# Slot numbers of 8 bits in place of words in the count stage of a graph network kernel

## The chip, the core and the metric

The kernel runs on one core of a Trainium2 chip. The metric is the time of the whole program on that core in microseconds (us), the median of three runs. TensorE is called PE here, VectorE DVE, ScalarE ACT, GpSimd POOL, SyncE SP. Each engine has a sequencer, which also runs the register instructions of its program; in the rows these stand under the engine's name with a q behind it (PEldq is the sequencer of PE, which issues weight loads and matmuls both).

## What is computed

Four graph layers run one after the other on 3125 nodes of 128 features, over 103125 edges that are sorted by destination. The part that matters here is what all the first three layers share: a sum over the edges of a node.

```python
edge_index = jnp.stack([src, dst])
h = jnp.maximum(_layernorm(x, axis=-1), 0.0)
x = x + _L0_gnn_ref(h, edge_index, ...)     # segment_sum of gated messages
x = x + _L1_gnn_ref(h, edge_index)          # three rounds: segment_sum(x[src], dst) / count
x = x + _L2_gnn_ref(h, src, dst, ...)       # segment_sum(feat[src], dst) / degree, two linears
x = x + _L3_gnn_ref(h, edge_index, edge_attr_32, ...)   # attention over the edges
```

For the first three layers the kernel builds once a matrix of counts (how many edges run from node s to node d) and then multiplies with it. The stage that builds this matrix is the one that is changed.

## The kernel before

**Stages.** `tables` works out the index tables on DVE with a little help of PE. `count_matrix` builds the counts. Then come layer 0, layer 1, layer 2 (matmuls with the counts) and layer 3 (projection, attention over edge groups, feed-forward). A stage is a block, and the next begins when all engines have left it.

**The count stage.** The edges lie in 806 tiles of 128, the nodes in 625 windows of 5 destinations. A step takes one tile and one window; there are 1431 steps. DVE makes the one-hot operands of 16 steps with two comparisons (line 617): one of the source's low 7 bits, 128 wide, one of the pair of window place and high bits, 125 wide. PE multiplies the two, with 128 rows of weights and 125 columns (line 646), and adds the product into a slot of 128 columns in PSUM. Which slot is data: the window of a step depends on the edges. Eight steps are a stride (`STRIDE`), so there are 179 strides. PSUM has 32 slots, in four pairs of banks (`PAIRS`). Per stride PE first sends two matmuls with one column of zeros (line 624, `clear`), which reset a pair of banks ahead, and ACT reads one pair of banks out into the counts (line 653).

**Places in registers.** `CountTables.places` works out on DVE, at the end of the tables stage, for each step its slot offset in PSUM (slot number times 128 columns) and for each stride the pair to clear (pair number times 1024). They lie in `c_place`, for each three strides (`AHEAD`) 24 + 3 values and one of padding: 28 words of 32 bits. PE's sequencer reads those 28 words into 28 registers with one TENSOR_LOAD (line 114, called from `values`), 60 times in the stage. The registers hold for the three strides that follow. Before each matmul a register instruction (FUSED_REGOPS) turns the value into an address. For line 646 it has two operations, times 4 bytes and plus the base of PSUM; for line 624 three, plus 511 or 1023, times 4, plus the base. ACT loads its own words, one of a stride, 8 at a time (line 657).

**Order and waits.** Everything is written out, with no scheduler. PE waits before a stride j for the read-out of stride j-2 (`copied`), and before each second stride for the one-hots of DVE (`hots`). DVE may be three chunks of 16 steps ahead (`ring`). ACT waits for the matmuls of the stride (`counted`).

Of the kernel before, what the change touches and what calls it, by code (L numbers as in the profile page):

```python
# [7 lines left out]
BF16 = mybir.dt.bfloat16  # L8
I32 = mybir.dt.int32
I16 = mybir.dt.int16  # L10
ALU = mybir.AluOpType
ACT = mybir.ActivationFunctionType
AX = mybir.AxisListType
ENGINE = mybir.EngineType
# [13 lines left out]
SLOT = 128  # L28
STRIDE = 2 * IN_BANK
PAIRS = 4  # L30
AHEAD = 3
F16_SCALE = 4096.0

# [112 lines left out]
class Path:  # L147
# [29 lines left out]
    def vector(self, e, v):  # L177
# [7 lines left out]
        e.wait_ge(v.sem, v.at(t))  # L185
        e.tensor_tensor(ends[:, :], ends[:, :], self.tile_no[:, :], ALU.add).then_inc(*v.up())
        t = v.n
# [25 lines left out]
class CountTables:  # L213
# [7 lines left out]
    def __init__(self, k, scope):  # L221
        s = k.s
        n, cols = s.csteps, s.nb * s.w
        self.k = k

        def sb(name, shape, dt=F32):
            return k.sb(scope, name, shape, dt, "right")
        self.key, self.low = sb("c_key", [P, n + 1], F16), sb("c_low", [P, n + 1], F16)

        self.fetches = -(-s.strides // AHEAD)
        self.words = -(-AHEAD * (STRIDE + 1) // 4) * 4
        self.place = sb("c_place", [1, self.fetches, self.words], I32)
        self.out = sb("c_out", [1, self.fetches * AHEAD], I32)
        self.lows, self.keys = sb("low_table", [P, P, 2], F16), sb("key_table", [P, cols, 2], F16)

    def stage(self, scope):
        k, s, n = self.k, self.k.s, self.k.s.csteps
        self.kb = -(-s.tiles // P)
        self.last = s.tiles - (self.kb - 1) * P  # L240
        self.cuts = [(lo, min(n, lo + 397)) for lo in range(0, n, 397)]
        kb, tiles = self.kb, s.tiles

        def sb(name, shape, dt=F32):
            return k.sb(scope, name, shape, dt)
        self.src, self.dst = sb("src_rows", [P, 2, kb, P], I32), sb("dst_rows", [P, 2, kb, P], I32)
        self.tile_no, self.step = sb("tile_no", [P, tiles]), sb("step", [P, 16])
        self.iota, self.far = sb("iota", [P, P]), sb("far", [P, s.nb * s.w])
        self.number = sb("number", [P, n], F16)
        self.part = sb("part", [P, 2, kb, P], I32)  # L250
        self.diff = sb("diff", [P, 4, kb, P], F16)
        self.dst_diff = sb("dst_diff", [P, kb, P])
        self.end, self.ends = sb("end", [P, kb], I32), sb("ends", [P, kb])
        self.before = sb("before", [P, kb, n], F16)
        self.shifts, self.near = sb("shifts", [P, n]), sb("near_key", [P, 2, 397])
        self.ones = sb("ones", [P, 1], F16)
        strides = self.fetches * AHEAD
        whole = strides * STRIDE
        self.window = sb("c_window", [1, whole], I32)
        self.fill, self.early = sb("c_fill", [1, strides], I32), sb("c_early", [1, strides])  # L260
        self.clear, self.pair, self.column = (sb(x, [1, strides], I32) for x in ("c_clear", "c_pair", "c_column"))
        self.blank, self.dst_here, self.src_here, self.numbers_here, self.tables_here = (k.flag(x) for x in (
            "c_blank", "c_dst_here", "c_src_here", "c_numbers_here", "c_tables_here"))
        self.before_ready, self.summed, self.lows_kept, self.emptied = (k.flag(x) for x in (
            "c_before", "c_summed", "c_lows_kept", "c_emptied"))
        self.v = k.flag("c_vector")
# [91 lines left out]
    def places(self, e):  # L358

        s, v = self.k.s, self.v
        assert STRIDE * PAIRS == 32 and SLOT == 128
        wide = STRIDE * s.w
        every = AHEAD * STRIDE
        e.memset(self.place[:, :, every + AHEAD:], 0).then_inc(*v.up())
        e.tensor_scalar(self.place[:, :, 0:every], self.window[:, :].rearrange("p (a b) -> p a b", b=every),
                             STRIDE * PAIRS - 1, 7, ALU.bitwise_and, ALU.logical_shift_left).then_inc(*v.up())
        e.tensor_scalar(self.fill[:, :], self.window[:, ::STRIDE], 3, None, ALU.logical_shift_right).then_inc(*v.up())
        t = v.n
        e.wait_ge(v.sem, v.at(t))  # L370
        for to, more in ((self.clear, 1), (self.pair, PAIRS - 1)):
            e.tensor_scalar(to[:, :], self.fill[:, :], float(more), None, ALU.add).then_inc(*v.up())
        e.tensor_scalar(self.early[:, :], self.fill[:, :], 1.0, float(wide * (s.fills - 1)),
                                 ALU.is_lt, ALU.mult).then_inc(*v.up())
        t = v.n
        e.wait_ge(v.sem, v.at(t))
        e.tensor_scalar(self.place[:, :, every:every + AHEAD], self.clear[:, :].rearrange(
            "p (a b) -> p a b", b=AHEAD), PAIRS - 1, 10, ALU.bitwise_and, ALU.logical_shift_left).then_inc(*v.up())
        e.tensor_scalar(self.pair[:, :], self.pair[:, :], PAIRS - 1, 16, ALU.bitwise_and, ALU.logical_shift_left).then_inc(*v.up())
        e.scalar_tensor_tensor(self.early[:, :], self.fill[:, :], float(wide), self.early[:, :],  # L380
                                        ALU.mult, ALU.add).then_inc(*v.up())
        t = v.n
        e.wait_ge(v.sem, v.at(t))
        e.tensor_scalar(self.column[:, :], self.early[:, :], -float(wide), None, ALU.add).then_inc(*v.up())
        t = v.n
        e.wait_ge(v.sem, v.at(t))
        e.tensor_tensor(self.out[:, :], self.column[:, :], self.pair[:, :], ALU.bitwise_or).then_inc(*v.up())
# [30 lines left out]
def tables(k, c):  # L418
# [6 lines left out]
    with ExitStack() as scope:  # L425
# [7 lines left out]
        k.e_rel = k.dram("e_rel", (P, 4 * s.padded))  # L433
        k.e_rel_rows = k.dram("e_rel_rows", (s.padded, 2 * wide), I16)

# [149 lines left out]
def count_matrix(k, c, counts, room):  # L585
# [4 lines left out]
    s, w = k.s, k.s.w  # L590
    keep, ring, cols = c.KEEP, 3, s.nb * s.w
# [3 lines left out]
    with ExitStack() as scope:  # L595
        def sb(name, shape, dt=F32):
            return k.sb(scope, name, shape, dt)
        lows = room.bitcast(F16)[:, 0:ring * keep * P].rearrange("p (r n v i) -> p r n v i", r=ring, n=keep // 2, i=2)
        keys = sb("keys", [P, ring, keep // 2, cols, 2], F16)
        none = sb("none", [P, 512], F16)  # L600
        consts, hots, cleared, counted, copied = (k.flag(x) for x in (
            "count_constants", "hots", "cleared", "counted", "copied"))
        flat = k.psum[:, :, :].rearrange("p b n -> p (b n)")

        with k.nc.Block() as block:
            @block.vector
# [14 lines left out]
            @block.tensor  # L621
            def _(e):
                def clear(bank):
                    return e.matmul(bank, none[:, 0:P], none[:, 0:1], start=True, stop=True, skip_group_check=True)
                words = c.place[0:1, :, :].rearrange("p a b -> p (a b)")
                last_slot = (STRIDE * PAIRS - 1) * SLOT
                e.wait_ge(consts.sem, consts.at(1))
                for i in range(BANKS):
                    e.matmul(k.bank[i], none[:, 0:P], none[:, :], start=True, stop=True, skip_group_check=True)
                    last = clear(k.bank[i][:, 511:512])  # L630
                last.then_inc(*cleared.up())
                for j in range(s.strides):
                    if j % AHEAD == 0:
                        at = j // AHEAD * c.words
                        fetched = k.values(ENGINE.PE, words, at, at + c.words, last_slot)
                    place = fetched[j % AHEAD * STRIDE:(j % AHEAD + 1) * STRIDE]
                    ahead = fetched[AHEAD * STRIDE + j % AHEAD].with_bounds(min_val=0, max_val=(PAIRS - 1) * 1024)
                    if j >= 2:
                        e.wait_ge(copied.sem, copied.at(j - 1))
                    for i in range(2):  # L640
                        clear(flat[:, 512 * i + 511:][:, bass.ds(ahead, 1)])
                    if j % per == 0:
                        e.wait_ge(hots.sem, hots.at(2 * (j // per) + 2))
                    for i in range(j * STRIDE, min(s.csteps, (j + 1) * STRIDE)):
                        hot = (slice(None), i // keep % ring, i % keep // 2, slice(None), i % 2)
                        last = e.matmul(flat[:, bass.ds(place[i - j * STRIDE], cols)], lows[hot], keys[hot], start=False, stop=True,  # L646
                                        skip_group_check=True)
                    last.then_inc(*counted.up())

# [1530 lines left out]
```

## Time and profile before

| what | value |
|---|---|
| three runs, median (lowest to highest) | 2661.04 us (2653.04 to 2667.34) |
| the profiled execution, by the clock of the runs | 2660.26 us |
| its span in the trace | 2658.5 us |
| PE busy, of the span | 1727.1 us (65%) |
| DVE busy | 1524.0 us (57%) |
| ACT busy | 940.4 us (35%) |
| the count stage, from the first to the last clearing matmul | 75.3 to 414.6 us |

Busy time counts work on data only. Register instructions and the loading of registers are not in it, so an engine whose sequencer is reading registers looks idle; such a gap is put down either to "issue" or to whichever semaphore happened to come last. The trace still has these instructions, and a view of one source line shows their number and their duration.

### The profile page before, as it was taken

How to read it: one execution, taken by the hardware profiler on the slowest of the kernel's cores; microseconds unless marked ns; L12 is line 12 of the kernel's file. 1: busy time of each engine (PE TensorE's matmuls, PEld its weight loads, DVE VectorE, ACT ScalarE, POOL GpSimd, SP SyncE). 2: the span in 40 equal slices, each digit the busy share in tenths (PEclk: the TensorE clock that was granted, in tenths of full speed). 3: DMA queues.
4: the chain of work that ended last, by engine and by line, in shares of the span. 5: the costliest groups of instructions: out<-in, count | busy, mean ns of one | idle time of the engine just before them, and what ended most of it. 6: DMA issues, size and time to landing. Idle time of an engine off the chain costs nothing. (4 is left out here: it accounts for less than half of the span.)

```text
span 2658.5 us, 34091 instructions
## 1 busy us (share of the span) xinstructions
PE 1727.1 (65%) x10020; PEld 1399.0 (53%) x10020; DVE 1524.0 (57%) x3280; ACT 940.4 (35%) x2179; POOL 891.8 (34%) x871
## 2 busy tenths in 40 slices
PE   4666665995599777443566665756565566666665
PEld 2455553553488665232455554645455555555663
DVE  5666664774432333843565665656656666566786
ACT  0455554673334131300223323324233233242455
POOL 1000000000000000076666655666656566566600
PEclk9555555998799889677777867778878777787777
DMA  2000001000024000132323323333223233223211
GB/s 65 20 1 1 1 1 27 1 0 24 25 59 126 1 1 8 43 97 70 80 72 77 79 70 75 73 75 78 75 75 79 76 78 78 70 71 82 69 26 29
DMA packets 131762, 136.86 MB, mean 51 GB/s; under 512 B 28321, under 2 KB 101634, under 8 KB 131586
## 3 DMA queue, kind: packets, MB, share of 16 engines
q0 software_dynamic: 27776, 60.71, 10.1%
q1 hardware_dynamic: 103810, 73.98, 9.8%
q8 instruction: 90, 1.47, 0.2%
q14 instruction: 86, 0.70, 0.1%
HBM read 129.67 MB, written 4.92 MB: 51 GB/s over the span
## 5 line engine op out<-in xcount | busy, mean ns | idle before, releaser
L1618 POOL DMA_INDIRECT rows<-x_l,src x856 | 875.7, 1023 | 966.4 <-DMA rows<-L_gnn_b 449.7
L1686 PE MATMUL psum<-both,node_hot 128*128 128x144 f32 x1712 | 326.1, 349 | 324.8 <-DVE both L1880 216.1
L1686 PEld LDWEIGHTS psum<-both,node_hot 128*128 128x128 f32 x1712 | 287.3, 238 | 353.4 <-issue 319.8
L1633 PE MATMUL psum<-w_e,edges 128*128 128x272 f32 x856 | 330.7, 472 | 132.5 <-issue 80.5
L1635 PEld LDWEIGHTS psum<-x_r,hot 128*128 128x128 f32 x1712 | 319.4, 226 | 100.3 <-issue 50.3
L1635 PE MATMUL psum<-x_r,hot 128*128 x1712 | 328.4, 316 | 43.0 <-issue 42.4
L1786 DVE TENSOR_SCALAR hot<-rel_row,place 128x512 f32<-128x512 int16 x214 | 103.9, 486 | 340.9 <-remote 289.5
L1743 ACT ACTIVATE apart<-iota,minus_rel 128x128 f32<-128x128 f32 x828 | 261.9, 386 | 0.1
L653 ACT ACTIVATE counts<-psum (+1 forms) x181 | 181.4, 1002 | 186.9 <-PE psum L646 117.0
L1898 DVE TENSOR_TENSOR acc<-acc,psum 128x144 f32 x428 | 128.7, 301 | 198.1 <-remote 135.4
L1633 PEld LDWEIGHTS psum<-w_e,edges 128*128 128x128 f32 x856 | 165.5, 233 | 140.5 <-issue 96.8
L1019 PE MATMUL psum<-halves,counts 128*128 128x257 f16 (+1 forms) x1875 | 214.0, 276 | 28.4 <-PEq L1036 24.5
L1039 POOL MEMSET halves<- 128x6425 f16 x1 | 5.5, 5456 | 651.6 <-SPq L1036 651.6
L1019 PEld LDWEIGHTS psum<-halves,counts 128*128 128x128 f16 (+1 forms) x1875 | 185.7, 99 | 56.8 <-issue 25.5
L646 PE MATMUL psum<-keys,x 128*128 128x125 f16 x1431 | 201.8, 285 | 0.5
L617 DVE TENSOR_TENSOR x<-low_table,c_low 128x2048 f16<-128x2048 f16 x90 | 109.6, 1218 | 123.2 <-PE psum L646 121.3
L1739 ACT ACTIVATE both<-weight 128x64 f32<-128x64 f32 x214 | 52.7, 246 | 344.8 <-remote 264.5
L646 PEld LDWEIGHTS psum<-keys,x 128*128 128x128 f16 x1431 | 149.0, 105 | 25.4 <-issue 1.5
L1793 DVE TENSOR_TENSOR z<-psum,rows 128x544 f32<-128x544 f32 x214 | 153.0, 715 | 9.1 <-issue 9.1
L1806 DVE TENSOR_REDUCE alpha<-z 128x32 f32<-128x544 f32 x214 | 152.5, 712 | 1.6 <-issue 0.5
L1799 DVE SCALAR_TENSOR_TENSOR z<-z,att 128x512 f32<-128x512 f32 x214 | 146.6, 685 | 1.1
L1880 DVE TENSOR_TENSOR both<-rows,weight 128x512 f32<-128x512 f32 x214 | 143.9, 680 | 3.5 <-issue 2.6
(299 smaller groups left out, 2101.9 us busy)
## 6 DMA issues: line engine op xcount, KB each, us to landing
rel_row<-e_rel_rows SPq DMA_DIRECT2D x107, 256.0 KB
rows<-x_l,src POOLq DMA_INDIRECT x856
edges<-edge_t SPq DMA_DIRECT2D x428, 32.0 KB
edge_part<-edge_t SPq DMA_DIRECT2D x22, 576.0 KB
x_r<-x_l SPq DMA_DIRECT2D x1, 1632.0 KB
new<-e_new_before SPq DMA_DIRECT2D x12, 128.0 KB
new<-e_new_behind SPq DMA_DIRECT2D x12, 128.0 KB
x_l<-xl SPq DMA_DIRECT2D x4, 340.0 KB
```

What stands on the lines that cost most here:

```text
L646: last = e.matmul(flat[:, bass.ds(place[i - j * STRIDE], cols)], lows[hot], keys[hot], start=False, stop=True, skip_group_check=True)
L653: return e.activation(counts[:, :, column].rearrange("p h (a j) -> p h a j", j=w), pair.rearrange("p b (a n) -> p (b a) n", n=SLOT)[:, 0:f ...
L1019: last = e.matmul(ps, counts[:, i, b * P:b * P + rows], halves[:, i, :], start=i == 0, stop=i == s.nb - 1)
L1618: e.indirect_dma_start(rows[:, g % ring, j * ROW:(j + 1) * ROW], None, k.xl, bass.IndirectOffsetOnAxis(ap=src[:, at:at + 1], axis=0)).then ...
L1633: e.matmul(pair[:, j // 2, :], edges[:, r, :], w_e[:, j:j + 2, :].rearrange("p j f -> p (j f)"), start=True, stop=False)
L1635: final = e.matmul(pair[:, j // 2, j % 2 * ROW:(j % 2 + 1) * ROW], hot[:, two, j * P:(j + 1) * P], node_rows[j // 2], start=False, stop=j ...
L1686: final = e.matmul(to, near_hot[:, at, j, :], both[:, at, j, :], start=j % 2 == 0, stop=j % 2 == 1)
L1743: e.activation(apart[:, u % 2, j, :], iota[:, :], ACT.Abs, bias=minus_rel[:, 4 * u + j:4 * u + j + 1]).then_inc(*far.up())
L1793: e.tensor_tensor(z[:, g % 2, :].rearrange("p (b f) -> p b f", b=2), pair_of(g), rows_at(g).rearrange("p (b f) -> p b f", b=2), ALU.add).t ...
L1799: e.scalar_tensor_tensor(heads, heads, 0.0, att_of(k, 4), ALU.max, ALU.mult).then_inc(*leaky.up())
L1806: e.tensor_reduce(alpha[:, b.two, :, g - b.first, :], z[:, g % 2, :].rearrange("p (v h c) -> p v h c", v=4, h=HEADS), AX.X, ALU.add).then_ ...
L1880: e.tensor_tensor(both[:, at, :, 0:D].rearrange("p v (h c) -> p v h c", c=CH), rows_at(u).rearrange("p (v h c) -> p v h c", v=4, h=HEADS)[ ...
```

## The change

`c_place` becomes a tile of bytes. A step has its slot number, 0 to 31, a stride the number of its pair, 0 to 3, and three strides take 24 + 3 bytes and 5 of padding (`FETCH` = 32). PE loads 32 bytes with one TENSOR_LOAD, into 32 registers, again 60 times. The multiplication by 128, or by 1024, that the table held is now made by the sequencer, since PSUM is seen as slots and as pairs.

```diff
+FETCH = 32
...
-        self.words = -(-AHEAD * (STRIDE + 1) // 4) * 4
-        self.place = sb("c_place", [1, self.fetches, self.words], I32)
+        assert AHEAD * (STRIDE + 1) <= FETCH
+        self.place = sb("c_place", [1, self.fetches, FETCH], U8)
...
-        e.tensor_scalar(self.place[:, :, 0:every], self.window[:, :].rearrange("p (a b) -> p a b", b=every),
-                             STRIDE * PAIRS - 1, 7, ALU.bitwise_and, ALU.logical_shift_left).then_inc(*v.up())
+        e.tensor_scalar(self.slot[:, :], self.window[:, :], STRIDE * PAIRS - 1, None, ALU.bitwise_and).then_inc(*v.up())
...
-        e.tensor_scalar(self.place[:, :, every:every + AHEAD], self.clear[:, :].rearrange(
-            "p (a b) -> p a b", b=AHEAD), PAIRS - 1, 10, ALU.bitwise_and, ALU.logical_shift_left).then_inc(*v.up())
+        e.wait_ge(v.sem, v.at(u))
+        e.tensor_copy(self.place[:, :, 0:every], self.slot[:, :].rearrange("p (a b) -> p a b", b=every)).then_inc(*v.up())
+        e.tensor_scalar(self.clear[:, :], self.clear[:, :], PAIRS - 1, None, ALU.bitwise_and).then_inc(*v.up())
...
+        e.tensor_copy(self.place[:, :, every:every + AHEAD], self.clear[:, :].rearrange("p (a b) -> p a b", b=AHEAD)).then_inc(*v.up())
...
-        flat = k.psum[:, :, :].rearrange("p b n -> p (b n)")
+        slots = k.psum[:, :, :].rearrange("p b (a n) -> p (b a) n", n=SLOT)
+        pairs = k.psum[:, :, :].rearrange("p (a i) n -> p a (i n)", i=2)
...
-                        clear(flat[:, 512 * i + 511:][:, bass.ds(ahead, 1)])
+                        clear(pairs[:, bass.ds(ahead, 1), 512 * i + 511])
...
-                        last = e.matmul(flat[:, bass.ds(place[i - j * STRIDE], cols)], lows[hot], keys[hot], start=False, stop=True,
+                        last = e.matmul(slots[:, bass.ds(place[i - j * STRIDE], 1), 0:cols], lows[hot], keys[hot], start=False, stop=True,
```

In the built program the number of instructions of PE is the same. The FUSED_REGOPS of line 646 has three operations in place of two, that of the first `clear` of a stride four in place of three, that of the second three as before. On DVE the places are worked out with two instructions more. At the end of the tables stage DVE has, before the change:

```order
L365 MEMSET c_place 1x60
L366 TENSOR_SCALAR c_place<-c_window 1x60x24
L368 TENSOR_SCALAR c_fill<-c_window 1x180
L372 TENSOR_SCALAR c_clear<-c_fill 1x180
L372 TENSOR_SCALAR c_pair<-c_fill 1x180
L373 TENSOR_SCALAR c_early<-c_fill 1x180
L377 TENSOR_SCALAR c_place<-c_clear 1x60x3
L379 TENSOR_SCALAR c_pair<-c_pair 1x180
L380 SCALAR_TENSOR_TENSOR c_early<-c_fill,c_early 1x180
L384 TENSOR_SCALAR c_column<-c_early 1x180
```

And in the same place of DVE with the change:

```order
L367 MEMSET c_place 1x60x5
L368 TENSOR_SCALAR c_slot<-c_window 1x1440
L370 TENSOR_SCALAR c_fill<-c_window 1x180
L374 TENSOR_SCALAR c_clear<-c_fill 1x180
L374 TENSOR_SCALAR c_pair<-c_fill 1x180
L375 TENSOR_SCALAR c_early<-c_fill 1x180
L380 CAST c_place<-c_slot 1x60x24
L381 TENSOR_SCALAR c_clear<-c_clear 1x180
L383 TENSOR_SCALAR c_pair<-c_pair 1x180
L384 SCALAR_TENSOR_TENSOR c_early<-c_fill,c_early 1x180
L389 CAST c_place<-c_clear 1x60x3
L390 TENSOR_SCALAR c_column<-c_early 1x180
```

The arithmetic now goes into `c_slot` and `c_clear`, and two casts, of 1440 and of 180 numbers, carry the results into the byte tile.

## Rows read from the trace of the kernel before

**Rows 1.** Stretches of the program: start:end, busy us of each engine, granted clock, DMA share

```profile
core 0: us, PE busy (x) PEld busy (x) DVE busy (x) ACT busy (x) POOL busy (x), PEclk, DMA share, GB/s
0.00:75.00 75.00, 31.35 (x158) 15.36 (x158) 41.73 (x113) 3.16 (x5) 10.65 (x14) 0.90 0.26 74
75.00:417.00 342.00, 234.34 (x1805) 187.30 (x1805) 208.91 (x181) 180.99 (x180) 0.00 (x0) 0.50 0.00 1
417.00:640.00 223.00, 186.38 (x568) 107.44 (x569) 141.78 (x269) 121.59 (x155) 0.00 (x0) 0.89 0.04 10
...
```

**Rows 2.** Groups of instructions, 77 to 418 us: busy, mean ns, idle before

```profile
line engine op names shapes xcount | busy us, mean ns | idle before us <-releasers
L646 PE MATMUL psum<-keys,x 128*128 128x125 f16 x1431 | 201.8, 285 | 0.5
L653 ACT ACTIVATE counts<-psum x179 | 180.0, 1005 | 186.8 <-PE psum L646 117.0 <-ACT counts L653 39.6 <-PE psum L624 30.2
L617 DVE TENSOR_TENSOR x<-low_table,c_low 128x2048 f16<-128x2048 f16 x88 | 107.8, 1225 | 122.9 <-PE psum L646 120.9
L617 DVE TENSOR_TENSOR keys<-key_table,c_key 128x2000 f16<-128x2000 f16 x89 | 106.2, 1193 | 0.0
```

**Rows 3.** Waits, same stretch: engine, line, releaser, us in total, times, longest

```profile
engine line waited for: us in total, times, longest us
DVE x L617 <- PE psum L646: 121.3, 70, 2.3
PEld psum L624 <- issue: 117.3, 64, 2.1
ACT counts L653 <- PE psum L646: 117.0, 69, 2.2
PE psum L624 <- ACT counts L653: 96.7, 54, 1.9
...
```

**Rows 4.** PE in order of time, one group of three strides

```profile
start us, us, engine line op out<-in xcount [idle before <-releaser]
282.60 0.31 PE L624 MATMUL psum<-none 128*128 128x1 f16 x2 [1.81 <-ACT counts L653]
282.85 1.11 PE L646 MATMUL psum<-keys,x 128*128 128x125 f16 x8
283.80 0.31 PE L624 MATMUL psum<-none 128*128 128x1 f16 x2
284.05 1.13 PE L646 MATMUL psum<-keys,x 128*128 128x125 f16 x8
285.02 0.31 PE L624 MATMUL psum<-none 128*128 128x1 f16 x2
285.27 1.13 PE L646 MATMUL psum<-keys,x 128*128 128x125 f16 x8
288.17 0.31 PE L624 MATMUL psum<-none 128*128 128x1 f16 x2 [1.78 <-issue]
```

**Rows 5.** Line 114, loading of registers, whole span: min/median/max ns

```profile
engine op xcount: duration ns min/median/max, first and last start us, forms
L114 PEldq TENSOR_LOAD <-c_place x60: 1871/1874/2061, 75.3 to 411.2; - x60
...
L114 PEldq TENSOR_LOAD <-regs x54: 333/591/612, 1128.2 to 2506.2; - x54
L114 DVEq TENSOR_LOAD <-regs x54: 343/597/843, 1130.2 to 2581.5; - x54
L114 ACTq TENSOR_LOAD <-c_out x23: 539/547/747, 74.8 to 393.6; - x23
```

**Rows 6.** Line 114, 393 to 394.5 us: the last load of ACT, of three words

```profile
L114 ACTq TENSOR_LOAD <-c_out x1: 710/710/710, 393.6 to 393.6; - x1
```

**Rows 7.** Register instructions of lines 646, 624, 1635 (each view of its line)

```profile
L646 PEldq FUSED_REGOPS  x1431: 37/37/42, 77.7 to 415.3; - x179
L624 PEldq FUSED_REGOPS  x358: 46/51/51, 77.5 to 414.5; - x179
L1635 PEldq FUSED_REGOPS  x428: 46/46/51, 1135.4 to 2543.5; - x143
```

**Rows 8.** PE at the start of the stage: stretches, then order of time

```profile
80.60:83.60 3.00, 1.24 (x13) 0.88 (x10) 3.00 (x4) 2.15 (x3) 0.00 (x0) 1.00 0.00 0
90.00:93.00 3.00, 3.00 (x27) 2.51 (x25) 0.90 (x2) 1.44 (x2) 0.00 (x0) 0.50 0.00 0
...
80.77 1.07 PE L646 MATMUL psum<-keys,x 128*128 128x125 f16 x8
...
84.07 1.10 PE L646 MATMUL psum<-keys,x 128*128 128x125 f16 x8
```

**Rows 9.** ACT in order of time

```profile
285.89 1.00 ACT L653 ACTIVATE counts<-psum  x1 [0.63 <-ACT counts L653]
287.25 1.00 ACT L653 ACTIVATE counts<-psum  x1 [0.35 <-ACT counts L653]
289.83 1.01 ACT L653 ACTIVATE counts<-psum  x1 [1.57 <-PE psum L646]
```

**Rows 10.** DVE in order of time, places at the end of the tables stage

```profile
53.92 0.85 DVE L366 TENSOR_SCALAR c_place<-c_window 1x1440 int32<-1x1440 int32 x1
54.70 0.30 DVE L368 TENSOR_SCALAR c_fill<-c_window 1x180 int32<-1x180 int32 x1
55.64 0.24 DVE L377 TENSOR_SCALAR c_place<-c_clear 1x180 int32<-1x180 int32 x1
55.80 0.23 DVE L379 TENSOR_SCALAR c_pair<-c_pair 1x180 int32<-1x180 int32 x1
56.60 0.33 DVE L387 TENSOR_TENSOR c_out<-c_column,c_pair 1x180 int32<-1x180 int32 x1
56.95 0.67 DVE L491 CAST dstf<-e_dst 128x1024 f32<-128x1024 int32 x1
```

## What the change does to the time: the prediction

> **What bounds the kernel now.** I read the stretches first, since the change touches one stage only. [rows 1] has the count stage, 75 to 417 us: 342 us in which PE is busy for 234, DVE for 209 and ACT for 181, with next to no DMA. No engine is full, so something between them must set the pace. The groups [rows 2] name the work: 1431 matmuls of line 646, the one-hots of line 617, the read-outs of line 653. DVE idles 122.9 us before its one-hots and ACT 117.0 us for the matmuls, so both wait for PE. The waits [rows 3] say what PE waits for: 96.7 us "for ACT", 117.3 us for "issue" in its weight loads. That pair is the trap of this profile: both go back to one gap.
>
> The order of time [rows 4] shows it. Three strides run from 282.60 to 286.4, with 1.20 and 1.22 us from one to the next, and then PE stands still until 288.17; 5.57 us for the group. The gap stands once in three strides, exactly where the program has its TENSOR_LOAD of `c_place`. The view of line 114 gives its duration: 60 loads, 1.871 to 2.061 us, median 1.874 [rows 5]. 1.874 and some 0.06 us around it make the 1.93 us that the third stride is longer than the others (288.17 - 285.02 = 3.15 against 1.22). So 59 of 60 loads, 59 x 1.874 = 110.6 us, are a bare stall of PE's sequencer; the first, at 75.3 us, lies beside the clearing of the banks. ACT is no cause: its three read-outs of a group follow at 1.36 us (287.25 - 285.89) [rows 9], 4.08 us of the 5.57.
>
> Inside a stride, too, the sequencer is the limit and not the array. A matmul of line 646 takes 285 ns by the record [rows 2] but a new one starts each 0.12 us: (1.11 - 0.285) / 7 = 0.118 [rows 4]. At the start of the stage, with the clock granted at 1.0 (2.4 GHz), eight matmuls fill 1.07 us; after the fall to 0.5 (1.2 GHz) 1.10 us [rows 8]. The matmuls alone would shrink by half between these clocks. What doesn't follow the clock is the sequencer's turn: register instruction, weight load, matmul. So each nanosecond that is added to a register instruction there counts in full.
>
> **The change, part by part.** First, register arithmetic. One operation more in 1431 FUSED_REGOPS of line 646 and in 179 of line 624. Line 646's has two operations and takes 37 ns at least and in the median; line 1635's, on the same sequencer, has three and takes 46 [rows 7]. One operation is 9 ns. It is on the path by the reading above: 1431 x 9 = 12.9 us, and 179 x 9 = 1.6 us, though no row has four operations. The sum is +14.5 us. Bounds: at least 0, should the array hide it after all, and at most 51 - 37 = 14 ns each, 22.5 us.
>
> Second, the work on DVE. Arithmetic on 1440 words stays (0.85 us, the next starts 0.78 later), and a cast of 1440 numbers to bytes is added; I give it the same 0.78 us. The one-operation arithmetic on 180 words and its cast replace one instruction: one more, at 0.16 to 0.24 us [rows 10]. DVE goes straight on to line 491 and what follows, for which the end of the stage waits. Nothing hides it: +1.0 us. The bounds: 0.5, should the casts run at half of that, and 2.1, twice what the rate of line 491's cast gives (0.67 us for 1024 numbers, 0.94 for 1440) and the short one.
>
> Third, the load, and here the trace has no row: nobody loads bytes. Its price must come from how the loads of words behave [rows 5], and I take the duration apart. PE reads 28 words in 1.874 us; of its 54 loads of `regs` in the attention stage 53 are of 8 words, 0.591 in the median, and the last is of 4, 0.333 (the minimum). From 4 to 8 that is 0.258 us, from 8 to 28 1.283 / 5 = 0.257 for each four. So a load is about 0.075 us and 0.257 us for each 16 bytes, exact to a few ns. ACT's last load, of three words (179 is 22 x 8 + 3), breaks the line: 0.710 us [rows 6], more than the 0.547 of its loads of eight. A remainder of less than 16 bytes seems to be read word by word: (0.710 - 0.075) / 3 = 0.212 each. Sixteen bytes at once cost hardly more than a lone word. The likeliest reading is one round trip of some 0.2 us for each 16 bytes, and then a little for each register. 32 bytes are two such trips.
> The lower end is the 8 words of today: also 32 bytes, two trips, 0.591 us. The upper end of this reading adds the registers: 24 more than in that row, at (0.257 - 0.212) / 3 = 0.015 us each, 0.36 us, so 0.95 us. I take 0.75, about the middle, since one register operation costs 9 ns elsewhere on this sequencer (24 x 9 = 0.22 us, which gives 0.81) and the first number may hold some of it already. The saving is 59 x (1.874 - 0.75) = 66.3 us; at the ends 75.7 and 54.5.
>
> **The sum.** -66.3 + 14.5 + 1.0 = -50.8 us. From the profiled execution, 2660.26 us (which is within 1 us of the median, 2661.04), 2609.5, say 2610. With 0.591 it is 2600, with 0.95 2621.
>
> **What is late next.** The group of three strides becomes 5.57 - 1.12 + 27 x 0.009 = 4.69 us. ACT needs 3 x 1.36 = 4.08, and its own load of 0.547 us every eight strides adds 0.2: 4.28. DVE needs 1.225 + 1.193 = 2.42 us for two strides, 3.63 for three. Both still fit, and PE may be nearly two strides ahead of ACT. At the lower end of the load the group is 4.53, and ACT is covered by 0.25 us only. A higher granted clock, should the denser stage bring one, gives nothing here, by [rows 8]. Nothing later changes: layer 0 starts earlier by the same amount, with the same work; where its clock rises may shift by a few us, which I leave to the range.
>
> **Rivals.** *Each register costs its own share.* The same rows can be read as 0.064 us a register, (1.874 - 0.591) / 20, with four handled in one go whatever their size. Then 32 registers take 2.13 us: 59 x 0.257 = +15.2 us, and with +15.5 of the other parts the kernel is slower, 2691. It decides at one number: the load of the new form must be under 1.874 - 15.5 / 59 = 1.61 us for any gain. For it speaks that all rows are linear in registers as well as in bytes, since all are of words; against it the three words at 0.710, which show that it is not the count of registers that is paid.
>
> *Bytes leave the quick way altogether.* If only whole words are read 16 bytes at a time, and each byte is fetched as ACT's lone words are, 32 fetches make 0.075 + 32 x 0.212 = 6.86 us: 59 x 4.99 = +294 us, with the rest 2970. The place is the same gap of PE. For it speaks [rows 6]; it needs that the type, and not the length, decides. Runtime: NRT & Kernel Launch (Instruction fetch mechanics) of the Trainium skill speaks against this change in that way: it gives about 200 ns for each register loaded, "even for bulk". The 28 words at 1.874 us, 67 ns each, don't bear this out; ACT's three at 0.710, 237 ns each, nearly do. An estimate by that page, 32 x 0.2 = 6.4 us, would be 2943.
>
> *The gain is eaten by the next in line.* If the load fell to 0.591 and ACT's latency after each stride, not its throughput, came up, the group would end at some 4.8 in place of 4.53 us, which gives back 16 us: 2616. That is inside the first forecast. *No effect*: a load of 1.4 to 1.8 us, half by bytes and half by registers, would balance the added arithmetic, within 13 us of 2661.
>
> **How the numbers follow.** By bytes, with the eaten gain: 0.63, all of it faster by over 0.5% (about what a measurement of this kernel can tell from no change). By registers: 0.14, slower by 1.2%. Byte by byte: 0.16, far slower. Balanced: 0.07, of which I put 0.05 within 0.5% and 0.01 on each side. That makes 0.64 faster, 0.05 same, 0.31 slower. The likeliest case has 2597 to 2625 to itself, with the ends of the load, the bounds of the arithmetic and a few us of spread between executions. To leave out no more than 2 in 10 the range must take in the case by registers, up to 2696; the case byte by byte is left out.
>
> **What would show it.** Line 114 of PE with 60 loads of 32 bytes: 0.6 to 0.95 us confirms the reading by bytes, 2.13 that by registers, near 6.9 that byte by byte. The register instruction of line 646 at 46 ns, the first clearing matmul's at 60, matmuls 0.127 us apart. The gap of PE before each third stride at 0.65 to 0.9 us where it was 1.78. The waits of DVE and ACT for PE smaller by about 60 us each. About 1 us more on DVE before line 491. The forecast is wrong where the load is outside of these, or where the matmuls are still 0.118 apart, which would mean that the added operation is hidden.

## The result: slower by 13%, and the profile after

The changed kernel takes 3013.13 us in the median of four runs (3004.26 to 3020.41) against 2664.19 us (2653.04 to 2667.74): a ratio of 1.132, 95% interval 1.127 to 1.136. The forecast was 2610, in a range that ended at 2696. What happened is the rival "bytes leave the quick way altogether", which had a chance of 0.16 and put the time at 2970 us.

The stretches of the changed kernel, with the same columns as [rows 1], show where: before the count stage 1.1 us more, in it 692.3 us in place of 342, in layer 0 behind it the same 223 us.

```profile
core 0: us, PE busy (x) PEld busy (x) DVE busy (x) ACT busy (x) POOL busy (x), PEclk, DMA share, GB/s
0.00:76.40 76.40, 31.73 (x159) 15.51 (x160) 43.26 (x116) 3.16 (x5) 10.64 (x14) 0.87 0.24 73
76.40:768.70 692.30, 246.67 (x1805) 188.24 (x1805) 208.75 (x180) 181.35 (x181) 0.00 (x0) 0.50 0.00 1
768.70:991.70 223.00, 186.42 (x569) 107.62 (x570) 141.96 (x270) 121.22 (x155) 0.00 (x0) 0.89 0.04 10
```

The view of line 116 (line 114 of before, [rows 5]) has the cause in one line: each of 60 loads of 32 bytes takes 7.522 us where 28 words took 1.874. The loads of eight words by the same engine are unchanged, at 0.591 us.

```profile
engine op xcount: duration ns min/median/max, first and last start us, forms
L116 PEldq TENSOR_LOAD <-c_place x60: 7517/7522/7708, 76.4 to 756.8; - x60
...
L116 PEldq TENSOR_LOAD <-regs x54: 332/591/609, 1480.4 to 2864.8; - x54
```

In order of time PE shows the same pattern as [rows 4], three strides and a gap, only that the gap is 7.43 us long and not 1.78, and the group 11.47 us and not 5.57. The rows here, and the waits below, put it down to "issue".

```profile
303.42 0.31 PE L631 MATMUL psum<-none 128*128 128x1 f16 x2 [7.43 <-issue]
303.67 1.18 PE L653 MATMUL psum<-keys,x 128*128 128x125 f16 x8
304.70 0.31 PE L631 MATMUL psum<-none 128*128 128x1 f16 x2
304.95 1.19 PE L653 MATMUL psum<-keys,x 128*128 128x125 f16 x8
306.00 0.31 PE L631 MATMUL psum<-none 128*128 128x1 f16 x2
306.27 1.15 PE L653 MATMUL psum<-keys,x 128*128 128x125 f16 x8
314.89 0.18 PE L631 MATMUL psum<-none 128*128 128x1 f16 x1 [7.46 <-issue]
```

The waits of the stage, as in [rows 3]: what DVE and ACT wait for PE has grown from about 120 us to 460 and 470 us. Both do the same work as before and wait longer for it; they are no cause (DVE is busy for 208.8 us of the stage where it was 208.9, ACT for 181.4 where it was 181.0 [rows 1]).

```profile
ACT counts L660 <- PE psum L653: 470.0, 98, 8.1
DVE x L624 <- PE psum L653: 461.7, 87, 8.0
PEld psum L631 <- issue: 447.8, 63, 7.8
PE psum L631 <- issue: 436.0, 59, 7.6
```

The register instructions that got an operation more came out as costed: 46 ns in line 653, all of them, and 60 ns (four operations) in the first of the two of line 631. The second has three operations as before and takes 46 ns where it took 51 [rows 7]. Matmuls of line 653 start 0.128 us apart, (1.18 - 0.285) / 7, where it was 0.118 and 0.127 was forecast.

```profile
L653 PEldq FUSED_REGOPS  x1431: 46/46/46, 84.5 to 766.7; - x179
...
L631 PEldq FUSED_REGOPS  x358: 46/53/60, 84.2 to 765.8; - x179
```

And at the start of the stage the first load, which lay hidden beside the clearing of the banks at 2.06 us, now outlasts it. The clearing ends near 80.1 us, the first stride comes at 84.32:

```profile
79.93 0.21 PE L631 MATMUL psum<-none 128*128 128x1 f16 x1
84.32 0.29 PE L631 MATMUL psum<-none 128*128 128x1 f16 x2 [4.18 <-issue]
84.55 1.16 PE L653 MATMUL psum<-keys,x 128*128 128x125 f16 x8
85.57 0.31 PE L631 MATMUL psum<-none 128*128 128x1 f16 x2
```

### The profile page after: what moved, and what is told of

Same layout as the page of the kernel before. It is cut to its first block and busy times, and to the rows that moved or that the text cites. A ratio compares the mean times of both kernels' runs of the same rounds, so it can differ in the third digit from the quotient of the medians.

```text
span 3013.8 us, 34095 instructions
## 1 busy us (share of the span) xinstructions
PE 1729.4 (57%) x10020; PEld 1392.6 (46%) x10020; DVE 1527.5 (51%) x3282; ACT 940.8 (31%) x2179; POOL 888.7 (29%) x871
## 5 line engine op out<-in xcount | busy, mean ns | idle before, releaser
L660 ACT ACTIVATE counts<-psum (+1 forms) x181 | 181.4, 1002 | 538.3 <-PE psum L653 477.7
L631 PE MATMUL psum<-none 128*128 128x1 f16 x366 | 56.6, 184 | 443.5 <-issue 443.5
L631 PEld LDWEIGHTS psum<-none 128*128 128x128 f16 x366 | 38.1, 104 | 463.9 <-issue 455.4
L653 PE MATMUL psum<-keys,x 128*128 128x125 f16 x1431 | 212.8, 285 | 0.5
```

Of the source, the lines that this page charges most:

```text
L653: last = e.matmul(slots[:, bass.ds(place[i - j * STRIDE], 1), 0:cols], lows[hot], keys[hot], start=False, stop=True, skip_group_check=True)
L660: return e.activation(counts[:, :, column].rearrange("p h (a j) -> p h a j", j=w), pair.rearrange("p b (a n) -> p (b a) n", n=SLOT)[:, 0:f ...
```

## Experiments

The first four kernels ran on one chip with the kernel before, at 2390.76 us there, and the next three on one where it took 2676.93 us. The chips differ behind the count stage (the second stretch of e1 below has 1971.5 us against 2241 us in the trace of the kernel before), so each kernel is compared with the kernel before as measured on its own chip, and stages by their length. The one trace of the kernel before comes from its first measurement. That its count stage is as long on the chips of the experiments is taken from the changed kernel and e4, which have the same stage to 0.1 us (692.3) on two chips. e2, e3, e4 and e7 were run once each, so they are judged by the length of the stage and of the load first. From the first load to the end of the last read-out the count stage takes 342.1 us before and 692.3 us after.

### e1: the arithmetic without the bytes

```diff
-FETCH = 32
+FETCH = 28
...
-        self.place = sb("c_place", [1, self.fetches, FETCH], U8)
+        self.place = sb("c_place", [1, self.fetches, FETCH], I32)
```

> The changed kernel, but its table of slot numbers is of 28 words of 32 bits for three strides and not of 32 bytes: the added register operation and the added work of DVE alone. Theory (the loss is all in the load of bytes): the load of PE is back at 1.874 us, register instructions of line 653 at 46 ns, the stage 12 us longer than before, the whole some 13 us over the kernel before (ratio 1.005). Rival (the new addressing or the layout of the tiles costs as well): 30 us or more over it.

2404.3 us, ratio 1.0068 (1.0049 to 1.0087), 13.5 us in the medians: that is the price of all that was changed but the type of the load and its last four numbers (28 for 32). The load of PE, and the two stretches (the count stage and all behind it):

```profile
L116 PEldq TENSOR_LOAD <-c_place x60: 1869/1872/2064, 76.7 to 424.4; - x60
```

```profile
76.70:430.70 354.00, 246.48 (x1805) 186.88 (x1805) 208.66 (x180) 181.40 (x181) 0.00 (x0) 0.50 0.01 1
430.70:2402.20 1971.50, 1413.41 (x8057) 1163.91 (x8057) 1277.52 (x2987) 757.37 (x1993) 893.46 (x857) 0.85 0.27 66
```

The stage takes 354.0 us, 11.9 more than before. The register instructions account for it: line 653's are all at 46 ns, where 1074 of before took 37 and 357 took 42 (the first two of each stride, counted in the trace), so 1431 x 7.75 = 11.1 us; in line 631 179 went from 51 to 60 and 179 from 51 to 46, together 0.7 us. The added operation is in full on PE's path, and the other 338 us of the stage hang on the load of 32 bytes.

### e2 and e3: more registers, and a remainder

```diff
-        self.words = -(-AHEAD * (STRIDE + 1) // 4) * 4
+        self.words = 32
```

> The kernel before, with 32 words loaded in place of 28, as many registers as the changed kernel. Theory (the type decides, words go in pieces of 16 bytes): a load of 2.131 us, the whole 15 us over the kernel before. Rival (32 registers in one load are too many for the quick way): a load near 7.5 us, the whole 340 us over.

```diff
-                        fetched = k.values(ENGINE.PE, words, at, at + c.words, last_slot)
+                        fetched = k.values(ENGINE.PE, words, at, at + AHEAD * (STRIDE + 1), last_slot)
```

> The kernel before, its 27 words loaded without the word of padding; nothing reads the 28th. Theory (24 words go in six pieces of 16 bytes, three words one by one): 0.075 + 6 x 0.257 + 3 x 0.235 = 2.32 us a load, the whole 27 us over the kernel before. Rival (one remainder sends the whole load the slow way): 0.075 + 27 x 0.235 = 6.4 us, the whole some 270 us over.

2405.33 and 2413.56 us, one run each, 14.6 and 22.8 over the kernel before. The loads, of e2 and then of e3:

```profile
L114 PEldq TENSOR_LOAD <-c_place x60: 2127/2130/2317, 76.6 to 427.4; - x60
```

```profile
L114 PEldq TENSOR_LOAD <-c_place x60: 2338/2342/2547, 75.5 to 438.4; - x60
```

2.130 us, where 2.131 was expected: 32 registers are not too many, and eight pieces of 0.257 with 0.075 around them hold to 0.001 us. The stage is 15.2 us longer (357.2). And 27 words take 2.342 us, longer than 28 or 32. Three single words cost 2.342 - 0.075 - 6 x 0.257 = 0.725 us, 0.242 each, and the quick pieces stay quick. The reading that the prediction drew from ACT's three words [rows 6], a remainder one by one, was right, at 0.242 and not 0.212 each. The stage is 27.5 us longer (369.6).

### e4: numbers of 16 bits

```diff
-        self.place = sb("c_place", [1, self.fetches, FETCH], U8)
+        self.place = sb("c_place", [1, self.fetches, FETCH], I16)
```

> The changed kernel with a table of 32 numbers of 16 bits (64 bytes) for three strides. Theory (all that is not a word of 32 bits is fetched number by number): 7.52 us a load, the same time as the changed kernel, near 3013 us. Rival (only bytes are slow, by their width): 64 bytes in four pieces, 1.10 us, near 2630 us. A cost that follows the bytes at the slow rate would give twice 7.5 us.

2742.87 us in one run, 352.1 over the kernel before (the changed kernel was 348.9 over its own), with a stage of 692.3 us, the same as with bytes.

```profile
L116 PEldq TENSOR_LOAD <-c_place x60: 7517/7521/7702, 78.7 to 759.1; - x60
```

Twice the bytes, the same time: the price is by number, and a half word is as slow as a byte. With e2 it is not the 32 registers that make the load slow. What is left besides the type is where the load starts: e7 and e5 below take that up.

### e7: words that start off a border of 16 bytes

```diff
-        self.words = -(-AHEAD * (STRIDE + 1) // 4) * 4
+        self.words = 29
...
-                        fetched = k.values(ENGINE.PE, words, at, at + c.words, last_slot)
+                        fetched = k.values(ENGINE.PE, words, at, at + 28, last_slot)
```

> The kernel before with rows of 29 words of which 28 are loaded, so that three of four loads start off a border of 16 bytes. Theory A (a quick piece is 16 bytes from wherever the load starts): 1.874 us for all, no change. Theory B (a quick piece is an aligned one): 6 aligned pieces and 4 single words, 0.075 + 6 x 0.257 + 4 x 0.235 = 2.56 us, in 45 of 60 loads, 31 us over. Theory C (an unaligned start sends the whole load the slow way): 6.7 us in 45 loads, some 215 us over.

2893.04 us in one run, 216 over: it came out as Theory C has it. A quarter of the loads, those that start on a border, are at 1.88 us (the very first of the stage at 2.07), and 45 are at 6.60, whether they start 4, 8 or 12 bytes behind a border:

```profile
L114 PEldq TENSOR_LOAD <-c_place x60: 1875/6600/6627, 76.1 to 619.6; - x60
```

45 x 4.726 = 212.7 us; the stage is 212.4 longer. So the slow way is open to words too: not only the type, but the start decides for the whole load, while a short end costs its own three words only. 28 words take 6.600 us and 32 bytes take 7.522, 0.2357 and 0.2351 us for each number. That the price is so nearly the same speaks for one and the same slow way; two loads do not prove it.

### e5: the compact table, loaded as words

```diff
-                words = c.place[0:1, :, :].rearrange("p a b -> p (a b)")
+                words = c.place[0:1, :, :].rearrange("p a b -> p (a b)").bitcast(I32)
...
-                        at = j // AHEAD * FETCH
-                        fetched = k.values(ENGINE.PE, words, at, at + FETCH, last_slot)
+                        at = j // AHEAD * FETCH // 4
+                        packed = k.values(ENGINE.PE, words, at, at + FETCH // 4, (1 << 29) - 1)
+                        fetched = [((packed[n // 4] >> (8 * (n % 4)) if n % 4 else packed[n // 4]) % 256 if n % 4 < 3 else packed[n // 4] >> 24).with_bounds(min_val=0, max_val=last_slot) for n in range(FETCH)]
```

> The byte table of the changed kernel, but its 32 bytes are loaded as 8 words of 32 bits, and each number is taken out of its word in the register instruction, by a remainder of 256, a division, or both. 
2718.36 us, ratio 1.0172 (1.0126 to 1.0219): 41 us slower than the kernel before, outside of both expectations. The load, then the register instructions of lines 654 and 631, then PE in order of time:

```profile
L116 PEldq TENSOR_LOAD <-c_place x60: 587/590/778, 77.1 to 462.1; - x60
...
L654 PEldq FUSED_REGOPS  x1431: 83/122/152, 79.2 to 466.2; - x179
...
L631 PEldq FUSED_REGOPS  x358: 52/85/138, 77.9 to 464.8; - x179
```

```profile
300.12 0.32 PE L631 MATMUL psum<-none 128*128 128x1 f16 x2 [0.55 <-issue]
300.43 1.66 PE L654 MATMUL psum<-keys,x 128*128 128x125 f16 x8
302.02 0.33 PE L631 MATMUL psum<-none 128*128 128x1 f16 x2
302.35 1.69 PE L654 MATMUL psum<-keys,x 128*128 128x125 f16 x8
303.96 0.33 PE L631 MATMUL psum<-none 128*128 128x1 f16 x2
304.32 1.65 PE L654 MATMUL psum<-keys,x 128*128 128x125 f16 x8
306.68 0.32 PE L631 MATMUL psum<-none 128*128 128x1 f16 x2 [0.71 <-issue]
```

The same 32 bytes come in 0.590 us, as the prediction had hoped of them at best, and the gap of PE is down to 0.55 to 0.71 us. The tile is that of the changed kernel, declared and filled by the same lines, and the loads start at the same places in it. They are quick here, and by e7 a load that starts off a border of 16 bytes is not. So the changed kernel's loads were not slow for their start, and what is left is the type in which the load reads the tile. With e4 and e2 this settles the cause. But a register instruction with both a remainder and a division takes some 134 ns, with one of them 84 to 108 in nearly all cases, where it was 37 before and 46 in the changed kernel: the strides are 1.9 us long and not 1.2. The stage is 48.9 us longer (391.0); the loads gave 59 x 1.284 = 75.8 us, so the arithmetic took about 125 us. Added up in the trace, the register instructions of the two lines take 125.6 us more than before. The rival put such an operation at 27 ns, which was too little.

### e6: two offsets in a word

```diff
-AHEAD = 3
+AHEAD = 6
+HALF = AHEAD // 2
...
-        self.words = -(-AHEAD * (STRIDE + 1) // 4) * 4
+        self.words = -(-HALF * (STRIDE + 1) // 4) * 4
...
+        for h, to in enumerate((self.place[:, :, 0:every], self.upper[:, :, 0:every])):
+            e.tensor_scalar(to, of[:, :, h, :], STRIDE * PAIRS - 1, 7 + 16 * h,
+                            ALU.bitwise_and, ALU.logical_shift_left).then_inc(*v.up())
...
+        e.tensor_tensor(self.place[:, :, 0:every], self.place[:, :, 0:every], self.upper[:, :, 0:every],
+                        ALU.bitwise_or).then_inc(*v.up())
...
+                    if j % AHEAD < HALF:
+                        place, ahead = [x % 65536 for x in place], ahead % 65536
+                    else:
+                        place, ahead = [x >> 16 for x in place], ahead >> 16
```

> The kernel before with two offsets of 16 bits in each word: 28 words for six strides, 30 loads in place of 60. A register instruction has one operation more, a remainder of 65536 or a division by it. Theory: 30 x 1.93 = 58 us saved, 1610 x 9 ns = 14.5 us and 1 us on DVE added, 42 us under the kernel before. Rival (the operation is 27 ns): 1610 x 27 ns = 43 us added, 14 us under it.

2669.12 us, ratio 0.9969 (0.9947 to 0.9990): a small gain, 8 us in the medians and 3 to 14 by the interval. The load and the register instructions of lines 663 and 635:

```profile
L115 PEldq TENSOR_LOAD <-c_place x30: 1870/1874/2066, 76.3 to 403.4; - x30
...
L663 PEldq FUSED_REGOPS  x1431: 62/73/81, 78.8 to 412.8; - x179
...
L635 PEldq FUSED_REGOPS  x358: 51/67/107, 78.5 to 411.8; - x179
```

Half of the loads are gone, and the register instruction of line 663 went from 37 to 73 ns in the median: the added operation is mostly 30 ns (67, the division) or 37 ns (74, the remainder), above even the rival. The stage is 338.3 us, 3.8 shorter: 30 x 1.93 = 58 us saved, and 54 given back, by which the register instructions of the two lines are longer in the trace (46.6 + 7.1).

## Why the prediction was wrong, point by point

**What bounds the stage** held. The 60 loads are a bare stall of PE's sequencer, and 59 loads count in full, as it said: 59 x 0.256 = 15.1 us against 15.2 in e2, 59 x 0.468 = 27.6 against 27.5 in e3, 59 x 5.648 = 333.2 of the 338.3 us between e1 and the changed kernel. Nearly all of the rest there is the first load. It was hidden, and that holds for one that gets shorter; at 7.7 us it outlasts the clearing of the banks, and the first stride begins 4.5 us later after it starts (84.55 - 76.4 against 78.95 - 75.3).

That the sequencer sets the 0.118 us of a matmul, and not the array, is a matter of a few ns, which the prediction did not see: the first eight of the kernel before, whose register instructions had run during the clearing of the banks, start mostly 0.106 us apart at a granted clock of 0.50 (the row below; single starts in the trace), while the median inside the strides is 0.115 before and 0.124 after. So there was 0.009 us between the two limits, and the added operation counts in full since it falls on the slower one.

```profile
78.95 1.00 PE L646 MATMUL psum<-keys,x 128*128 128x125 f16 x8
```

**The register arithmetic**, +14.5 us, was 11.8 (e1). The mechanism was right and the size a little high, since the median of 37 ns hid that a quarter of the instructions took 42, and since the second `clear` got faster by 5 ns. No run shows the reason of either.

**DVE**, +1.0 us, was 1.1: line 497 starts at 58.01 us and not at 56.95 [rows 10]. The cast of 1440 numbers lasts 0.90 us and the next instruction starts 0.82 behind it, for the step of 0.78 that was assumed; the memset of bytes takes 0.31 us, where that of words took 0.11 (line 365 of before).

```profile
53.79 0.31 DVE L367 MEMSET c_place<- 1x300 uint8 x1
54.03 0.83 DVE L368 TENSOR_SCALAR c_slot<-c_window 1x1440 int32<-1x1440 int32 x1
...
55.72 0.90 DVE L380 CAST c_place<-c_slot 1x1440 uint8<-1x1440 int32 x1
...
57.23 0.28 DVE L389 CAST c_place<-c_clear 1x180 uint8<-1x180 int32 x1
...
58.01 0.67 DVE L497 CAST dstf<-e_dst 128x1024 f32<-128x1024 int32 x1
```

**The load** is the step that failed. The prediction took it apart correctly for words, 0.075 us and 0.257 for each 16 bytes, with the remainder one by one (e2, e3; from a border of 16 bytes, e7), and then wrote "32 bytes are two such trips". No row said that. All rows were of 32-bit words, and in them 16 bytes and four words are the same thing. The choice between them was made by the three words at 0.710 [rows 6], which do tell quick pieces from single fetches, but tell nothing of the type. The prediction named them for the third case too, and priced it from them. But they showed that a slow way exists, at some 0.2 us for each number, so that the only question was what sends a load there, and no row leaned to either answer. To give 0.16 to "byte by byte" and 0.63 to "by bytes" was a preference without a row. The load was forecast at 0.75 us and measured at 7.522, and the saving of 66.3 us became a loss of 337.7: 59 x 5.648 = 333.2, and 4.5 at the first load. What came after it in the prediction, whether ACT would be late next, was not put to the test, since the one run with a short load has longer strides (e5).

**The price of the slow way** was 6.86 us and is 7.52: with the same 0.075 us around it (7.522 - 0.075) / 32 = 0.233 us for each number, where the prediction had 0.212, from one load of another engine. 59 x 0.66 = 39 us, which is nearly all between the rival's 2970 and 3013. The rule of the Trainium skill that was quoted there (Runtime: NRT & Kernel Launch, Instruction fetch mechanics: about 200 ns for each register, "even for bulk") is about borne out for bytes, half words and words that start off a border of 16 bytes, at 235 ns (7.522 / 32). It is not for words from a border of 16 bytes, at 67 ns (2.130 / 32). The page speaks of loads from HBM; the table here lies in SBUF.

**The sum** by what was measured: 337.7 for the loads, 11.8 for the arithmetic, 1.1 on DVE, 350.6 us. The spans differ by 355.3. Of the remaining 4.7 us 4.0 lie behind the count stage (2245.1 us in place of 2241.1), where two executions of one kernel may differ as much (the four of the changed kernel span 16 us as a whole). The cause of these 4.7 us stays open.

## What to carry to other kernels

A load into registers is not priced by its bytes: ask whether it takes the quick way, and load words of 32 bits, from a border of 16 bytes, in fours. Where a sequencer sets the pace, put the arithmetic into the table, on the engine that has time, and count a remainder or a division in a register as three to seven multiplications (30 to 37 ns in e6 and 38 to 62 in e5, where one multiplication is 9). And where all rows agree with two laws, because in them two sizes (here bytes and words) never vary apart, the rows speak for neither: price both.

## What the runs showed of the hardware that was not expected

- TENSOR_LOAD on PE: 0.590 us for 8 words, 1.874 for 28, 2.130 for 32; 7.522 for 32 bytes, 7.521 for 32 half words.
- The same 28 words from a start off a border of 16 bytes: 6.600 us.
- Three words more than 24 cost 0.725 us, four more 0.257, with 24 words at 0.075 + 6 x 0.257 = 1.617 us, which is worked out and was not run.
- A register instruction of PE with two operations takes 37 to 42 ns, three 46 (51 in the `clear` of before), four 60 in one place. In e6 one with three takes mostly 67 ns with a division and 74 with a remainder for a multiplication, 21 and 28 more than 46; with both, in e5, it takes some 134.
- Matmuls of 128x125 f16 with a register address start 0.115 us apart at the half clock, where eight whose register instructions ran ahead start mostly 0.106 apart.
